# Small-head attention on one core: every matmul of the steps split into four column tiles of 128x32

## The reference

```python
qh = (q @ Wq.T + bq).reshape(B, Qlen, 16, 8).transpose(0, 2, 1, 3)
kh = (k @ Wk.T + bk).reshape(B, Klen, 16, 8).transpose(0, 2, 1, 3)
vh = (v @ Wv.T + bv).reshape(B, Klen, 16, 8).transpose(0, 2, 1, 3)
score = jnp.einsum('bhqd,bhkd->bhqk', qh, kh) / np.sqrt(8)
attn = jax.nn.softmax(score, axis=-1)      # layer 0 has a mask (all true here)
out = jnp.einsum('bhqk,bhkd->bhqd', attn, vh)
return out.transpose(0, 2, 1, 3).reshape(B, Qlen, 128) @ Wo.T + bo
```

## Time and profile before

| what | us |
|---|---|
| median of 3 runs | 2117.55 (2115.62 to 2126.2) |
| the profiled execution | 2118.41, span 2116.5 |
| PE busy / DVE / ACT / POOL | 1962.0 / 1417.7 / 1255.2 / 1096.5 |
| layer 0's steps, first to last `scores0` | 35.4 to 416.9 |
| layer 3's steps, first to last `scores0` | 1678.0 to 2055.5 |

### The profile page before, as it was taken

One profiled execution on the slowest core, in us unless ns is written; L12 is line 12 of the kernel. 1 busy time (PEld: TensorE's weight loads), 2 busy tenths in 40 slices (PEclk: granted clock), 3 DMA queues, 4 the chain that ended last, 5 costly groups with the idle time before them and its releaser, 6 DMA issues. The chain is left out here.

```text
span 2116.5 us, 52255 instructions
## 1 busy us (share of the span) xinstructions
PE 1962.0 (93%) x21121; PEld 1386.7 (66%) x21121; DVE 1417.7 (67%) x2766; ACT 1255.2 (59%) x2169; POOL 1096.5 (52%) x1176
## 2 busy tenths in 40 slices
PE   5999999965999799889999999999979699999996
PEld 3677777745787554656766766767745377777774
DVE  5677777768998454376666666666426577777774
ACT  5778778643676332276666666666403477777763
POOL 6566665204777374466776776776600453334400
PEclk8899999967999999899999999999989799999997
DMA  6544554323353120445655655554300454444420
GB/s 162 154 139 134 152 138 134 88 71 109 101 148 98 39 53 30 120 144 128 147 153 130 143 156 129 141 159 99 73 11 30 136 148 127 132 139 126 128 79 10
DMA packets 107536, 240.04 MB, mean 113 GB/s; under 512 B 47704, under 2 KB 56944, under 8 KB 107040
## 3 DMA queue, kind: packets, MB, share of 16 engines
q1 hardware_dynamic: 107296, 236.70, 41.0%
HBM read 155.38 MB, written 0.65 MB: 74 GB/s over the span
## 5 line engine op out<-in xcount | busy, mean ns | idle before, releaser
L1728 POOL TENSOR_SCALAR L2values<-L2values,L2value_stats 128x127 f32<-128x127 f32 x768 | 341.4, 462 | 0.0
L1635 PE MATMUL L2ps<-L2keys,L2qz 128*128 128x384 f32 x896 | 325.7, 505 | 5.6 <-DVE L2negmax L1836 5.6
L1652 PEld LDWEIGHTS L2ps<-L2work,L2values 32*128 32x128 f32 x6144 | 286.2, 186 | 64.8 <-issue 52.2
L1652 PE MATMUL L2ps<-L2work,L2values 32*128 32x224 f32 x6144 | 323.0, 357 | 5.8 <-DVE L2work L1846 5.8
L1846 DVE STREAM_TRANSPOSE L2work<-L2work 128x1568 f32<-128x1568 f32 x112 | 202.8, 1811 | 113.8 <-PE L2ps L1652 112.1
L1836 DVE CUSTOM_DVE_ANT_0 L2work<-L2ps,L2maskadd,L2big 128x1536 f32<-128x1536 f32 x112 | 203.6, 1818 | 94.7 <-PE L2ps L1635 94.7
L1635 PEld LDWEIGHTS L2ps<-L2keys,L2qz 128*128 128x128 f32 x896 | 159.7, 188 | 134.7 <-issue 28.6
L1779 ACT ACTIVATE L2work<-L2work,L2rinv 128x1536 f32<-128x1536 f32 x112 | 176.8, 1578 | 115.8 <-DVE L2rinv L1851 115.8
L1774 ACT ACTIVATE L2work<-L2work,L2negmax 128x1536 f32<-128x1536 f32 x112 | 176.2, 1573 | 109.5 <-DVE L2negmax L1836 109.4
L654 ACT ACTIVATE L3probsT<-L3ps 128x448 f32<-128x448 f32 x384 | 196.0, 547 | 70.9 <-PE L3ps L511 66.2
L654 ACT ACTIVATE L0probsT<-L0ps 128x448 f32<-128x448 f32 x384 | 198.0, 551 | 47.5 <-PE L0ps L511 46.3
(11 more groups left out here) (482 smaller groups left out, 3937.6 us busy)
## 6 DMA issues: line engine op xcount, KB each, us to landing
L2values<-in_ctx SPq DMA_DIRECT2D x192, 192.0 KB, 4.5
L0key_stack<-L0key_parts SPq DMA_DIRECT2D x192, 187.5 KB
L3key_stack<-L3key_parts SPq DMA_DIRECT2D x192, 187.5 KB
L0ctxT<-in_ctxT SPq DMA_DIRECT2D x16, 750.0 KB, 4.4
L1rawT<-in_ctxT SPq DMA_DIRECT2D x16, 750.0 KB, 6.5
L2mean_spread<-L_moments SPq DMA_DIRECT2D x16, 750.0 KB, 5.8
L3ctxT<-in_ctxT SPq DMA_DIRECT2D x16, 750.0 KB, 4.5
L2wqk<-L_moments SPq DMA_DIRECT2D x15, 750.0 KB, 7.9
```

Source lines behind the costliest of these rows:

```text
L1635: last = nc.tensor.matmul(PS[:, score_bank(m) + w, 0:NCH * BW], tile_rows(m), key_window(b, w), start=True, stop=True)
L1652: last = nc.tensor.matmul(PS[:, 4 + a, 0:RT * BW], V[a * BW:(a + 1) * BW, n, :], block_cells(a, b, n), start=n == 0, stop=n == BLOCKS - 1, ...
L1728: last = nc.gpsimd.tensor_scalar(x, x, VST[:, 1, w, b, c:c + 1], VST[:, 0, w, b, c:c + 1], ALU.mult, ALU.add)
```

## The change

A helper `narrow` issues one matmul as pieces of 32 output columns, each in its own tile of 128x32 of the array (`tile_position=(0, c)`). All matmuls of the steps go through it: `scores0`, `scores12`, S, K, V, M, R, Y. The products of values were already so. Nothing else is touched: same operands, banks, waits, semaphores and order of units. The semaphore is raised by the last piece. The matmuls outside the steps (layer norm transposes, query projection, bias) stay whole.

```diff
+            def narrow(out, lhsT, rhs, start=True, stop=True):
+                for c in range(0, lhsT.shape[1], 32):
+                    at = slice(c, min(c + 32, lhsT.shape[1]))
+                    last = nc.tensor.matmul(out[at], lhsT[:, at], rhs, start=start, stop=stop, tile_position=(0, c))
+                return last
+
...
-                nc.tensor.matmul(PS[0:TT, 0, 0:500], QS[0:SROWS, h % 4, tau, :], KS[0:SROWS, h % 4, tau, 0:500],
-                                 start=True, stop=True).then_inc(s.s0_filled, 1)
+                narrow(PS[0:TT, 0, 0:500], QS[0:SROWS, h % 4, tau, :], KS[0:SROWS, h % 4, tau, 0:500]).then_inc(s.s0_filled, 1)
...
-                    last = nc.tensor.matmul(PS[0:TT, c, 0:500], QS[0:SROWS, h % 4, tau, :],
-                                            KS[0:SROWS, h % 4, tau, c * 500:(c + 1) * 500], start=True, stop=True)
+                    last = narrow(PS[0:TT, c, 0:500], QS[0:SROWS, h % 4, tau, :], KS[0:SROWS, h % 4, tau, c * 500:(c + 1) * 500])
...
-                        last = nc.tensor.matmul(PS[:, bank, c * TT:(c + 1) * TT], KS[:, h % 4, tau, key_columns(4 * j + c)],
-                                                QS[:, h % 4, tau, :], start=True, stop=True)
+                        last = narrow(PS[:, bank, c * TT:(c + 1) * TT], KS[:, h % 4, tau, key_columns(4 * j + c)], QS[:, h % 4, tau, :])
...
-                    last = nc.tensor.matmul(PS[:, bank, 0:500], WQK[:, 1, :], CT[:, i % 3, j * 500:(j + 1) * 500],
-                                            start=True, stop=True)
+                    last = narrow(PS[:, bank, 0:500], WQK[:, 1, :], CT[:, i % 3, j * 500:(j + 1) * 500])
...
-                        last = nc.tensor.matmul(PS[:, bank, c * P:(c + 1) * P], CT[:, i % 3, key_columns(4 * j + c)],
-                                                WV[:], start=True, stop=True)
+                        last = narrow(PS[:, bank, c * P:(c + 1) * P], CT[:, i % 3, key_columns(4 * j + c)], WV[:])
...
-                        last = nc.tensor.matmul(PS[0:2 + NM, bank, tau * TT:(tau + 1) * TT], HL[:, i % 2, tau, :], IB[:],
-                                                start=True, stop=True)
+                        last = narrow(PS[0:2 + NM, bank, tau * TT:(tau + 1) * TT], HL[:, i % 2, tau, :], IB[:])
...
-                    last = nc.tensor.matmul(PS[:, bank, 0:TT], SEL[:], OS[:, i % 2, :], start=True, stop=True)
+                    last = narrow(PS[:, bank, 0:TT], SEL[:], OS[:, i % 2, :])
...
-                            last = nc.tensor.matmul(PS[:, bank, 0:Q], WO[:, h, x, :], Am[:, h, x * Q:(x + 1) * Q],
-                                                    start=h + x == 0, stop=h + x == 2)
+                            last = narrow(PS[:, bank, 0:Q], WO[:, h, x, :], Am[:, h, x * Q:(x + 1) * Q], h + x == 0, h + x == 2)
```

## The result

The changed kernel takes 2219.4 us (2211.47 to 2220.67, four runs) against 2118.04 for the kernel before beside it: ratio 1.0466, 95% interval 1.0444 to 1.0488. The forecast was 2048 us, with a range of 2015 to 2118. It was wrong, in sign too.

What follows compares the result with a forecast made beforehand. PE was taken as the bound, 24.5 us a batch; less 2.2, 0.55 and 0.92, plus a 1.14 VectorE wait, gives 21.95. 26 batches at 2.5 plus 5 take 70 us off 2118.4: 2048 us, range 2015 to 2118.

Steps and rivals of the forecast that it cites:

- What it adds: Four times as many S, score, K, V, R and Y matmuls cost nothing if the four pieces run side by side.
- Switches around `values`: Passages between whole array and column tiles at each `values` go: 0.27 us a step, 2.2 us a batch.
- Switches around M: Switches at M's matmuls, which have only 3 output columns, go: 0.27 us twice a batch, 0.55 us.
- fp32 loads: fp32 weight loads of Y, R, V and K in pieces load beside one another: 0.92 us a batch less.
- PE waits 1.14 once a batch for VectorE: Near M of t = 2, PE waits 1.14 us a batch for VectorE's row-maxima chain, which the change does not touch.
- ScalarE and the DMAs carry layer 0: ScalarE's 19.56 us a batch and the DMA share of 0.53 fit; at most some 0.5 us a batch lost if not.
- PE alone 20.8, a batch of 21.95: PE's own work falls from 24.5 to 20.8 us a batch; with the VectorE wait a batch takes 21.95 us.
- Rival 1: The array takes records no faster than in `values`, 24 ns each; S 0.38 us, kernel 2147 us; 12%.
- Rival 2: bf16 pieces stream at half rate, 9.8 us a batch more on S and scores; kernel 2277 us; 7%.
- Rival 3: The gaps around `values` are waits and no switches, so nothing goes: 2110 to 2118 us; 5%.
- Rival 4: VectorE does not hold PE up, so a batch takes 20.8 us and the kernel 2017 us; 6%.
- I am wrong if [...] a batch is over 24.5: Sign that would refute the forecast: a batch of 8 steps over 24.5 us, where about 22 us was expected.

Runs made afterwards that it cites:

- yr_near_two_narrow: Kernel before, with M, Y and R issued behind `values`, Y and R in pieces, and all matmuls cut only at t = 2 and 3: 2083.96 us, ratio 0.9851.
- m_beside_values: Kernel before, with M moved to t = 3 and 7 and issued right behind `values`, no matmul split: 2110.46 us, ratio 0.9952.
- s_one_piece: Changed kernel, with each S unit issuing only the first of its four pieces (incomplete results): 2065.63 us, ratio 0.974 against the kernel before.
- half_narrow: Kernel before, M behind `values`, pieces only from `values` of odd steps to the next, Y and R moved there: 2099.3 us, ratio 0.9901.
- few_stack_bytes: Changed kernel, copying only 8 of 1500 columns of the stacked keys from half batch 4 on: 2186.45 us, ratio 1.031 against the kernel before.
- mry_beside_values: Kernel before, with M, Y and R moved to t = 3 and 7 behind `values`, Y and R in pieces: 2133.23 us, ratio 1.0062.
- value_pairs: Kernel before, with the `values` of two steps issued together in every second step and K units moved: 2187.05 us, ratio 1.0318.
- all_beside_values: value_pairs and mry_beside_values together, against the kernel before: 2185.32 us, ratio 1.0306.

## Why the prediction was wrong

The step that failed is "What it adds": "If the four pieces run side by side, this costs nothing". They do run side by side; the instructions that issue them are not free. I counted the added matmuls (96 to 384, 24 to 96) and priced only their columns. The supply was in the page: 168 packets of 16 KB. From it, one block in 8.3 us before, and 2.3 times the records in a shorter batch would have asked for one in 22 x 256 / 1703 = 3.3 us. What a late block needs, some 3.5 us at the least, no row of before showed, since no block was late; it was an unpriced resource that more than doubled, and should have been a rival on the slower side with a wide price. In its place the runs show stalls at the borders of blocks of 5.9 us a batch (start to start, 150 to 415 us) and 0.8 us for the clock, which falls after some of them.

Point by point:
- *Switches around `values`, 2.2 a batch:* right. 0.20, 0.57 and 0.43 against the 0.29, 0.72 and 0.46 of the earlier trace rows. yr_near_two_narrow is a separate showing: two pairs fewer and two K units in pieces, 20 us less, where 0.27 x 2 x 32 = 17.
- *Switches around M, 0.55:* right in size; layer 3 of m_beside_values fell by 0.54.
- *fp32 loads, 0.92:* right. Y takes 0.39 (forecast 0.38, whole 0.89) and R 0.20 (forecast 0.19, whole 0.27). In the changed kernel's trace V behind S takes 0.88 (0.95 before) and K behind S 0.84 (0.90 before), so three V and one K give about the 0.25 that was put down for them.
- *PE waits 1.14 once a batch for VectorE:* mis-sized. In the changed kernel the waits for the row maxima add to 0.6 us in 280, since PE comes late anyhow. Where PE was faster (s_one_piece, layer 3) they are single waits of up to 1.4 us, 3.5 us in 280, so 0.3 a batch:

```profile
PE L3ps L473 <- DVE L3maxparts L808: 3.5, 11, 1.4
```

- *ScalarE and the DMAs carry layer 0, at most some 0.5 a batch:* hidden in the changed kernel, too small where PE is fast. In s_one_piece layer 0 stays 1.8 us a batch above layer 3, in part because PE stands behind ScalarE and the mask's load.
- *PE alone 20.8, a batch of 21.95:* the local work comes out near it. 150 to 430 us are 10.2 batches of 27.4; PE's two "issue" rows add to 43.5 us, 4.3 a batch, and the clock of 0.97 is 0.8 us a batch: 27.4 - 4.3 - 0.8 = 22.3. These rows count from the modelled end of the last matmul. From start to start the stalls are the 5.9 us above, and a full batch of 27.8 leaves 21.1, near PE's 20.8. So 5 to 7 us a batch of supply and clock took more than the gain on PE's own work.
- *Rival 1* (24 ns a record, S at 0.38, about 2147) came nearest in sign, but its place was wrong: S stays at 0.20. The limit is one on the mean: 4.1 us for 128 pairs of load and matmul, 32 ns a matmul. *Rival 2* (bf16 at half rate): refuted, a score matmul in pieces takes 0.21. *Rival 3*: refuted, the gaps went. *Rival 4* (VectorE does not hold it up): its condition nearly holds in layer 3 of s_one_piece, but the batch is 21.8 there and not 20.8; no run tries it alone.
- *"I am wrong if [...] a batch is over 24.5":* it is 27.4 (27.8 with K units).

What stays open: why a block's packet starts 1.1 us after PE's entry at one time and 3 or even 4.5 us (half_narrow's long stall) at another. The load of the other queues explains a part, as the groups above and few_stack_bytes show; the rest was only seen.

## What to carry to other kernels

Count instructions as a resource of their own when a change cuts work in pieces: the q8 line of the page over the span gives the time between blocks. On PE here stalls cost 0.6 us a batch at 4.9 us a block (half_narrow) and 5.9 us at 4.2 (the changed kernel), where they took the clock with them at times. Where the pieces avoid a cost at their border (here the passage between whole array and column tiles), first put the units of one kind side by side, which costs no instruction, and cut only what then still stands between two of them. Moving a unit moves the work of the other engines around it too: three of the kernels above (mry_beside_values, value_pairs, all_beside_values) lost more by PE's waits for VectorE and ScalarE than they gained on PE.

## What the runs showed of the hardware that was not expected

- PE's instructions come in packets of 16 KB per 256, each asked for about when PE enters the block before it. In the changed kernel a late block was there 3.5 to 5.75 us after that entry, in half_narrow once 7.1 us; with the DMA share at 0.19 the median was still 3.9.
- Of the eight stalls of over 2 us between 150 and 430 us, five (2.3 to 3.1 us) were followed by some 3 us at 1.2 GHz and three (2.2, 2.4 and 2.9 us) were not; none of the shorter ones was. So the length of a stall alone does not tell.
- Pieces of 32 columns in four tiles cost no more than the whole matmul, in bf16 too: 16 matmuls of 112 columns in 0.20 us, 12.5 ns each.
